# A third place for block outputs, denser last groups and fifteen moved steps in a hand-ordered mixture-of-experts kernel

## The chip, the cores and the metric

The kernel runs on one core of one Trainium2 chip. The metric is the device time of one execution in microseconds, as the median of three executions.

## What is computed

The input is 16 images of 128 channels and 32 x 32 points, in float32. Each image goes through a linear-attention block and then, point by point (token by token), through a mixture of eight experts:

```
x = x + rmsnorm(W_out @ attention(rmsnorm(ln_c(x))) + b_out)   # 4 heads of 32, softmax of q over dims, of k over tokens
t = tokens(x)                                                  # 16 * 1024 tokens of 128
probs = softmax(ln_t(t) @ gate_w + gate_b)                     # 8 experts
cw = the two largest probs of each token, at their experts, else 0
t = t + sum_e cw[:, e] * (gelu(ln_t(t) @ W1[e] + b1[e]) @ W2[e] + b2[e])   # 128 -> 256 -> 128
```

## The kernel before

**Stages.** An image is handled in three stages. In the *attention* (image n) the image is transposed, normed, multiplied and gated; VectorE ends it with `pick` (the two experts and their shares), `place` (row numbers: `row_of`, L936), and GpSimd then sends each token's normed row twice, to the region of each of its two experts in DRAM (`send`, L485: 16 indirect DMAs of 128 rows per image). Two images are a *group*; after the second, VectorE's `table` step (`make_plan`) computes from the counts which 256-row blocks there are and which expert each has. There are 8 groups and at most 23 blocks in each, 184 in all, numbered through: group 6 has 138 to 160, group 7 has 161 to 183. A *block* q goes through: load of rows and of the expert's weights by SyncE (`load_block`, L388 and L392), transpose on TensorE (`turn_block`, L1098), copy on ScalarE (`take_xt`, L588), `up` (L1107), two `gelu` (L594), `down` (L1117), `take_y` on VectorE (L991), store by SyncE to `rows_out` (`store_block`, L401). At last each image's rows come back: GpSimd's `fetch` (L499, 16 indirect DMAs per image), `weigh` on ScalarE (L581, two multiplications per pair of fetches), two adds per half image on VectorE (`add_rows`, L1000 and L1001), transposes on TensorE (`join`, L1027), a copy on ScalarE (`take_out`, L602), and a store of the half image (L407).

**The order.** Every engine runs one queue, written out by hand: a loop over quarter units (`ticks`) goes through all steps, and a step is put into its engine's queue at the unit that the tables give it. A unit delays nothing by itself; it only decides what stands before what in each queue. Steps of image n are at `START[n]` plus an entry of `PE_SLOT`, `ACT_SLOT`, `DVE_SLOT` or `POOL_SLOT`. Blocks are spread evenly over 42 units per image of the group (`block_slot`), and the steps of a block stand at 0 (`turn`), `XT`, `UP`, `UP + GELU`, `DOWN`, `DOWN + TAKE_Y` and `DOWN + 4` (store) behind its slot, its load 5 units ahead. Fetches are every 42 units per image (`fetch_slot`), the weighings 4 units behind a pair, adds and joins 6 and 8 units behind the last of a half.

**The waits around the change.** `rows_out` has `OUT_BUFS` places, taken by the groups in turn. Before the first store of group p, SyncE waits until every image of the group that had the place is added:

```
if j == 0 and p >= OUT_BUFS:
    wait(sp, s_added, 2 * FIRST[p - OUT_BUFS + 1])
```

A fetch of a group's first image waits until all the group's blocks are stored (`all_stored`). Six blocks are in flight (`RING`): the load of block q waits for the transpose of block q-6 (rows) and for `take_y` of block q-6 (weights). `y_rows` holds two images of fetched rows; a fetch waits for the adds of the image two before. A group's first block load waits for the sends of both its images and for the eight zero tails (`zero_tails`, L370), which wait for the plan.

Of the kernel before, what the change touches and what calls it, by code (L numbers as in the profile page):

```python
# [13 lines left out]
BATCH, CH, TOK = 16, 128, 1024  # L14
# [8 lines left out]
GROUPS = (2,) * 8  # L23
# [4 lines left out]
BLOCKS = tuple(2 * TOK * size // ROWS + EXPERTS - 1 for size in GROUPS)  # L28
BLOCK0 = tuple(sum(BLOCKS[:g]) for g in range(len(GROUPS)))
# [11 lines left out]

RING = 6
VALUES = 4
OUT_BUFS = 2
X1_RING, XF_RING, BACK_RING, YG_RING, OUT_RING = 8, 2, 3, 16, 4


PERIOD = 42
PACE = tuple((0.6, 0.6, 0.6, 0.8)[n] if n < 4 else 1.0 for n in range(BATCH))
START = tuple(int(4 * sum(PERIOD * PACE[m] for m in range(n))) / 4 for n in range(BATCH))  # L50
PE_SLOT = {"X0": 0.25, "X1": 2, "Q0": 15, "Q1": 16.1, "Q2": 16.45, "Q3": 17.55, "Q4": 18.65, "Q5": 20.25, "Q6": 20.85,
           "Q7": 21.95, "KT": 29, "KB": 31, "C": 38, "T0": 40.75, "CT": 41, "T1": 41.75, "M": 43, "F0": 45.75, "F1": 47,
           "F2": 47.5, "count": 84.5}
BANK_OF = {"X0": 2, "X1": 3, "Q0": 3, "Q1": 0, "Q2": 1, "Q3": 2, "Q4": 3, "Q5": 0, "Q6": 1, "Q7": 2, "KT": 0, "KB": 1,
           "C": 0, "T0": 1, "T1": 3, "CT": 0, "M": 0, "F0": 0, "F1": 1, "F2": 2, "count": 1, "Y0": 2, "Y1": 3}
ACT_SLOT = {"x_tok0": 1.75, "x_tok1": 3.25, "qkv": 15.75, "exp_q": 34, "exp_k": 34.75, "q_ch0": 41, "ctx_t": 42,
            "q_ch1": 42.5, "square0": 47, "square1": 48.25, "square2": 49, "exp": 76.5}
DVE_SLOT = {"bn1_0": 3.25, "bn1_1": 5.25, "stats1": 7, "inverse": 11.5, "gx": 25.5, "k_part": 27.25, "q_max": 28.75,
            "q_shift": 30.25, "k_max": 29.25, "k_shift": 31.75, "q_sum": 36, "q_norm": 39.75, "ctx": 40, "mix": 44.5, "root_first": 7.5, "root_a": 50.5, "root_b": 51.25,
            "norm0": 54.5, "norm1": 55, "norm2": 56, "x1": 58, "bn2_0": 59.5, "bn2_1": 59.75, "stats2": 61, "root2_a": 61.25, "root2_b": 61.5,  # L60
            "logits": 67.5, "scores": 72.75, "xf0": 78, "xf1": 79.75, "pick": 82.5, "place": 86.25, "table": 88.75}
POOL_SLOT = {"send": 92}
SEND_STEP = FETCH_STEP = 1.25

LOAD_X = -12
UP, DOWN = 5.25, 10.5
XT, GELU, TAKE_Y = 1, 1.5, 1.75
BLOCK_AFTER, FETCH_AFTER, FETCH_PHASE = 4, 13, 29
SCALE, ADD, JOIN = 4, 6, 8

# [5 lines left out]
def at(n, slot):  # L76

    return START[n] + round(4 * PACE[n] * slot) / 4
# [10 lines left out]
def group_of(n):  # L89

    return max(g for g in range(len(GROUPS)) if FIRST[g] <= n)
# [7 lines left out]
def start_slot(g):  # L99

    last = FIRST[g] + GROUPS[g] - 1
    ready = at(last, POOL_SLOT["send"]) + 2 * TILES * SEND_STEP + BLOCK_AFTER
    return ready if g == 0 else max(ready, start_slot(g - 1) + PERIOD * GROUPS[g - 1])


def block_slot(q):

    g = group_of_block(q)
    return start_slot(g) + int(4 * PERIOD * GROUPS[g] * (q - BLOCK0[g]) / BLOCKS[g]) / 4


def fetch_slot(n):

    g = group_of(n)
    done = start_slot(g) + PERIOD * GROUPS[g] + FETCH_AFTER
    phase = START[BATCH - 1] + FETCH_PHASE
    turn = phase + PERIOD * -((phase - done) // PERIOD)
    if n > FIRST[g]:
        return fetch_slot(n - 1) + PERIOD
    return turn if g == 0 else max(turn, fetch_slot(n - 1) + PERIOD)  # L120
# [9 lines left out]
def bank_order():  # L130

    names = list(PE_SLOT) + ["Y0", "Y1"]
    uses = [(at(n, PE_SLOT[name]), n, names.index(name), name) for n in range(BATCH) for name in PE_SLOT]
    uses += [(JOIN_SLOT[n][h], n, names.index(f"Y{h}"), f"Y{h}") for n in range(BATCH) for h in range(2)]
# [19 lines left out]
def build(nc, x, w_qkv, w_out, b_out, g_norm, g_out, gate_w, gate_b, w1, b1, w2, b2, out):  # L154
# [3 lines left out]
    rows_in = [nc.dram_tensor(f"rows_in{i}", [REGION, CH], F32, kind="Internal").ap() for i in range(2)]  # L158
    rows_out = [nc.dram_tensor(f"rows_out{i}", [MAX_BLOCKS * ROWS, CH], F32, kind="Internal").ap() for i in range(OUT_BUFS)]
    experts = nc.dram_tensor("experts", [EXPERTS * P, WROW], F32, kind="Internal").ap()  # L160

    with ExitStack() as ctx:
# [189 lines left out]
        def _(sp):  # L352
# [42 lines left out]
            def store_block(q):  # L395
                p = group_of_block(q)
                j, r = q - BLOCK0[p], q % RING
                if j == 0 and p >= OUT_BUFS:
                    wait(sp, s_added, 2 * FIRST[p - OUT_BUFS + 1])
                sp.wait_ge(s_yb, q + 1)  # L400
                sp.dma_start(rows_out[p % OUT_BUFS][j * ROWS:(j + 1) * ROWS, :].rearrange("(p s) c -> p (s c)", s=SUB),  # L401
                             yb[:, r, :, :].rearrange("p s c -> p (s c)")).then_inc(s_stored[r], 16)
# [51 lines left out]
        def _(pool):  # L454
# [35 lines left out]
            def fetch(n, i):  # L490
# [6 lines left out]
                if k == 0 and t % HT == 0:  # L497
                    wait(pool, s_added, n * 2 + t // HT + 1 - YG_RING // HT)
                pool.indirect_dma_start(  # L499
                    out=y_rows[:, r, k, :], out_offset=None, in_=rows_out[p % OUT_BUFS][0:BLOCKS[p] * ROWS, :],  # L500
                    in_offset=bass.IndirectOffsetOnAxis(
# [513 lines left out]
        def _(pe):  # L1015
# [14 lines left out]
            def attention(n, g):  # L1030
                for h in [h for h in range(2) if g == at(n, PE_SLOT[f"X{h}"])]:
                    if h == 0:
# [152 lines left out]
```

## Time and profile before

| what | us |
|---|---|
| median of 3 executions | 840.89 (838.65 to 841.69) |
| the profiled execution's own time | 844.55 |
| its span, first to last instruction | 842.7 |
| PE busy | 645.8 (77%) |
| DVE busy | 590.6 (70%) |
| ACT busy | 518.2 (61%) |
| POOL busy | 516.1 (61%) |

PE is TensorE, DVE VectorE, ACT ScalarE, POOL GpSimd, SP (SPq) SyncE, which issues the direct DMAs. A share of busy time is an average over the whole span. The mean granted clock of TensorE was 0.909 of full speed. DMA queues moved 173.45 MB, 206 GB/s in the mean. In the views of waits and of instructions in order of time, the text behind an arrow names what ended the idle time; "issue" is time in which the engine waited for nothing that the profile shows.

### The profile page before, as it was taken

The numbers are of one execution on the slowest core, as the hardware profiler recorded it, in microseconds if no ns is written. First come the engines' busy times: TensorE is split into PE (matmuls) and PEld (weight loads), VectorE is DVE, ScalarE is ACT, GpSimd is POOL, SyncE is SP. The second block draws the span as 40 slices with busy tenths as digits, with TensorE's granted clock in tenths as the row PEclk, the third lists the DMA queues.
The fourth block names the chain that finished last, engine by engine and source line by source line (L and its number), as shares of the span: only waits on it lengthen the run. The fifth ranks groups of instructions, "written<-read, shape, count | busy, mean of one in ns | idle before, by whom it ended". The sixth has DMA issues, their size and how long they took to land.

```text
span 842.7 us, 15573 instructions
## 1 busy us (share of the span) xinstructions
PE 645.8 (77%) x3979; PEld 537.8 (64%) x3979; DVE 590.6 (70%) x2185; ACT 518.2 (61%) x1382; POOL 516.1 (61%) x536
## 2 busy tenths in 40 slices
PE   4647546879998989898989898889888867778511
PEld 2425415767877787778777877787767656667400
DVE  4588996886889788978897989797978652222211
ACT  1433325666768696859695869587858563556532
POOL 1004464352177777777777777777777777776274
PEclk9877777999999999989999999899989989999855
DMA  6500035757687888787777787877777778889421
GB/s 167 143 25 29 26 122 158 218 170 230 196 248 226 269 247 258 221 264 248 244 243 250 252 246 249 254 234 240 244 247 235 237 226 283 258 250 305 138 78 56
DMA packets 120864, 173.45 MB, mean 206 GB/s; under 512 B 20792, under 2 KB 82888, under 8 KB 120776
## 3 DMA queue, kind: packets, MB, share of 16 engines
q1 hardware_dynamic: 103352, 138.65, 53.0%
q0 software_dynamic: 16384, 33.59, 13.5%
q8 instruction: 34, 0.56, 0.3%
q14 instruction: 54, 0.44, 0.2%
q10 hardware_dynamic: 1040, 0.21, 0.1%
HBM read 112.86 MB, written 62.14 MB: 208 GB/s over the span
## 4 chain that ended last, share of the span: by engine, by line
PE 37%; DVE 23%; issue 11%; POOL 11%; ACT 9%; DMA 4%; SPq 3%; POOLq 0%; DVEq 0%; ACTq 0%
PE y_ps L1117 10%; PE ab L1040 9%; PE h_ps L1107 8%; POOL y_rows L499 7%; POOL rows_in L485 3%; PE ab L1052 3%; DMA xb<-rows_in 3%; PE ab L1027 3%; PE t_ps L1098 2%; DVE yb L991 2%; ACT L544 2%; ACT y_rows L581 2%; PE ab L1074 2%; ACT qkv L548 1%; DMA y_rows<-rows_out,row_back 1%
## 5 line engine op out<-in xcount | busy, mean ns | idle before, releaser
L485 POOL DMA_INDIRECT rows_in<-xf_tok,row_of x256 | 258.2, 1008 | 219.9 <-DVE row_of L936 141.8
L499 POOL DMA_INDIRECT y_rows<-rows_out,row_back x256 | 255.6, 998 | 96.7 <-issue 77.2
L1117 PE MATMUL y_ps<-wb,hid 128*128 128x128 f32 x1472 | 207.1, 286 | 48.4 <-DVE yb L991 41.4
L1117 PEld LDWEIGHTS y_ps<-wb,hid 128*128 128x128 f32 x1472 | 193.1, 198 | 78.5 <-ACT hid L594 40.6
L1107 PE MATMUL h_ps<-xt,wb 128*128 128x256 f32 x736 | 200.7, 398 | 0.0
L594 ACT ACTIVATE hid<-h_ps,wb 128x256 f32<-128x256 f32 x368 | 160.0, 476 | 53.6 <-PE h_ps L1107 53.3
L991 DVE TENSOR_TENSOR yb<-y_ps,wb 128x256 f32<-128x256 f32 x184 | 76.9, 418 | 121.9 <-PE y_ps L1117 120.6
L1107 PEld LDWEIGHTS h_ps<-xt,wb 128*128 128x128 f32 x736 | 134.5, 200 | 19.5
L588 ACT ACTIVATE xt<-t_ps 128x256 f32<-128x256 f32 x184 | 71.0, 386 | 106.0 <-PE t_ps L1098 105.3
L1040 PE MATMUL ab<-wqkv_t,x_sb 128*128 128x392 f32 x256 | 107.5, 536 | 20.6 <-DVE gate_f L763 16.1
L581 ACT ACTIVATE y_rows<-y_rows,share 128x128 f32<-128x128 f32 x256 | 88.7, 403 | 34.0 <-DMA y_rows<-rows_out,row_back 34.0
L539 ACT ACTIVATE qkv<-ab,root 128x392 f32<-128x392 f32 x128 | 73.2, 588 | 51.6 <-PE ab L1040 26.6
L1098 PE MATMUL t_ps<-ident,xb 128*128 128x128 f32 x368 | 74.4, 285 | 20.8 <-DMA xb<-rows_in 17.8
L1040 PEld LDWEIGHTS ab<-wqkv_t,x_sb 128*128 128x128 f32 x256 | 48.3, 207 | 43.7 <-DVE gate_f L763 19.3
L1098 PEld LDWEIGHTS t_ps<-ident,xb 128*128 128x128 f32 x368 | 47.0, 146 | 30.9 <-DMA xb<-rows_in 22.7
L1000 DVE TENSOR_TENSOR x_tok<-x_tok,y_rows 128x512 f32<-128x512 f32 x32 | 22.2, 695 | 48.9 <-ACT y_rows L581 48.7
L1027 PE MATMUL ab<-ident,x_tok 128*128 128x128 f32 x128 | 22.3, 302 | 43.2 <-DVE x_tok L1001 43.2
L1052 PE MATMUL ab<-qkv 128*128 128x129 f32 x256 | 39.2, 316 | 12.7 <-ACT qkv L548 12.7
L1027 PEld LDWEIGHTS ab<-ident,x_tok 128*128 128x128 f32 x128 | 16.6, 155 | 48.3 <-DVE x_tok L1001 46.3
L1052 PEld LDWEIGHTS ab<-qkv 128*128 128x128 f32 x256 | 36.6, 227 | 16.2 <-ACT qkv L548 16.0
L1074 PE MATMUL ab<-mix,q_ch 128*128 128x136 f32 x256 | 37.2, 286 | 1.5 <-DVE mix L749 1.1
L760 DVE SCALAR_TENSOR_TENSOR x_tok<-ab,root,g_out_bc 128x128 f32<-128x128 f32 x128 | 37.1, 341 | 0.0
(174 smaller groups left out, 883.7 us busy)
## 6 DMA issues: line engine op xcount, KB each, us to landing
wb<-experts SPq DMA_DIRECT2D x184, 321.0 KB
xb<-rows_in SPq DMA_DIRECT2D x184, 128.0 KB, 3.5
rows_out<-yb SPq DMA_DIRECT2D x184, 128.0 KB
rows_in<-zeros SPq DMA_DIRECT2D x78, 128.0 KB, 2.3
x_sb<-in_x_dram SPq DMA_DIRECT2D x16, 512.0 KB, 4.9
out_dram<-out_sb SPq DMA_DIRECT2D x32, 256.0 KB, 4.0
rows_in<-xf_tok,row_of POOLq DMA_INDIRECT x256
y_rows<-rows_out,row_back POOLq DMA_INDIRECT x256, 4.0
```

Of the source, the lines that this page charges most:

```text
L485: pool.indirect_dma_start(out=rows_in[group_of(n) % 2], out_offset=bass.IndirectOffsetOnAxis(ap=row_of[:, n % X1_RING, k, t:t + 1], axis=0 ...
L499: pool.indirect_dma_start(out=y_rows[:, r, k, :], out_offset=None, in_=rows_out[p % OUT_BUFS][0:BLOCKS[p] * ROWS, :], in_offset=bass.Indir ...
L539: act.activation(qkv[:, t, 0:QKV], ab[:, BANK_OF[f"Q{t}"], 0:QKV], ACT.Copy, scale=root[:, 0, t:t + 1]).then_inc(s_qkv, 1)
L581: act.activation(y_rows[:, r, i, :], y_rows[:, r, i, :], ACT.Copy, scale=share[:, n % X1_RING, i, t:t + 1]).then_inc(s_scaled, 1)
L588: act.activation(xt[:, q % 2, :], t_ps[:, 0:ROWS], ACT.Copy).then_inc(s_xt, 1)
L594: act.activation(hid[:, q % 2, k, :], h_ps[:, q % 2, k * ROWS:(k + 1) * ROWS], ACT.Gelu, bias=wb[:, q % RING, B1_COL + k:B1_COL + k + 1]). ...
L991: dve.tensor_tensor(yb[:, q % RING, :, :], y_ps[:, 0:ROWS].rearrange("p (s c) -> p s c", c=CH), wb[:, q % RING, B2_COL:B2_COL + CH].unsque ...
L1040: pe.matmul(claim(n, f"Q{t}")[:, 0:QKV], x_sb[:, n % 2, t * P:(t + 1) * P], wqkv_t[:, :], start=True, stop=True).then_inc(s_qkv_mm, 1)
L1052: last = pe.matmul(bank[:, 0:P + 1], qkv[:, t, K_COL:V_COL], qkv[:, t, V_COL:QKV + 1], start=t == 0, stop=t == TILES - 1)
L1098: last = pe.transpose(t_ps[:, i * P:(i + 1) * P], xb[:, r, i, :], ident[:, :])
L1107: last = pe.matmul(h_ps[:, q % 2, k * ROWS:(k + 1) * ROWS], wb[:, r, k * P:(k + 1) * P], xt[:, q % 2, :], start=True, stop=True)
L1117: last = pe.matmul(y_ps[:, i * P:(i + 1) * P], hid[:, q % 2, k, i * P:(i + 1) * P], wb[:, r, HIDDEN + k * CH:HIDDEN + (k + 1) * CH], start ...
```

## The change

A third `rows_out` place; the blocks of the last two groups spread over 72 and 60 units instead of 84 each; the fetches of images 11 to 15 at units of their own (counted from `START[15]`) instead of 42 apart; and fifteen steps of the tables moved by 0.25 to 2 units.

```diff
-OUT_BUFS = 2
+OUT_BUFS = 3
-PE_SLOT = {... "Q0": 15, ... "count": 84.5}
+PE_SLOT = {... "Q0": 15.25, ... "count": 84.25}
-ACT_SLOT = {"x_tok0": 1.75, ...
+ACT_SLOT = {"x_tok0": 1.25, ...
-DVE_SLOT = {... "stats1": 7, "inverse": 11.5, ... "root_b": 51.25, ... "place": 86.25, "table": 88.75}
+DVE_SLOT = {... "stats1": 7.25, "inverse": 13.5, ... "root_b": 51.5, ... "place": 86, "table": 87.75}
+LAST_SPANS = (72, 60)
+SPAN = tuple(PERIOD * size for size in GROUPS[:-len(LAST_SPANS)]) + LAST_SPANS
+LAST_FETCH = {11: 111, 12: 133, 13: 159, 14: 180, 15: 200}
-XT, GELU, TAKE_Y = 1, 1.5, 1.75
+XT, GELU, TAKE_Y = 1.75, 1.75, 1.75
     (start_slot)
-    return ready if g == 0 else max(ready, start_slot(g - 1) + PERIOD * GROUPS[g - 1])
+    return ready if g == 0 else max(ready, start_slot(g - 1) + SPAN[g - 1])
     (block_slot)
-    return start_slot(g) + int(4 * PERIOD * GROUPS[g] * (q - BLOCK0[g]) / BLOCKS[g]) / 4
+    return start_slot(g) + int(4 * SPAN[g] * (q - BLOCK0[g]) / BLOCKS[g]) / 4
     (fetch_slot)
+    if n in LAST_FETCH:
+        return START[BATCH - 1] + LAST_FETCH[n]
-    done = start_slot(g) + PERIOD * GROUPS[g] + FETCH_AFTER
+    done = start_slot(g) + SPAN[g] + FETCH_AFTER
```

By the tables, the fetches of images 11 to 15 stood at units 684, 726, 768, 810 and 852 and now stand at 682, 704, 730, 751 and 771. Group 6 starts at unit 608.25 in both; group 7 at 692.25 before and at 687 now.

## Rows read from the trace of the kernel before

**Rows 1.** The page: shares of the span, and DMA issues with KB and landing.

```profile
PE 645.8 (77%) x3979; PEld 537.8 (64%) x3979; DVE 590.6 (70%) x2185; ACT 518.2 (61%) x1382; POOL 516.1 (61%) x536
...
wb<-experts SPq DMA_DIRECT2D x184, 321.0 KB
...
y_rows<-rows_out,row_back POOLq DMA_INDIRECT x256, 4.0
```

**Rows 2.** GpSimd in order of time: start, length, [idle time before, releaser].

```profile
227.49 0.96 POOL L485 DMA_INDIRECT rows_in<-xf_tok,row_of  x1 [31.90 <-DVE row_of L936]
...
652.40 1.00 POOL L485 DMA_INDIRECT rows_in<-xf_tok,row_of  x1 [1.04 <-issue]
...
693.50 1.00 POOL L485 DMA_INDIRECT rows_in<-xf_tok,row_of  x1 [0.30 <-issue]
...
713.82 0.97 POOL L499 DMA_INDIRECT y_rows<-rows_out,row_back  x1 [0.31 <-issue]
...
732.66 0.94 POOL L499 DMA_INDIRECT y_rows<-rows_out,row_back  x1 [0.30 <-issue]
734.93 0.94 POOL L499 DMA_INDIRECT y_rows<-rows_out,row_back  x1 [1.33 <-DMA rows_out<-yb]
...
774.60 0.94 POOL L499 DMA_INDIRECT y_rows<-rows_out,row_back  x1 [0.30 <-issue]
793.40 1.00 POOL L499 DMA_INDIRECT y_rows<-rows_out,row_back  x1 [17.86 <-DMA rows_out<-yb]
...
832.34 0.94 POOL L499 DMA_INDIRECT y_rows<-rows_out,row_back  x1 [0.30 <-issue]
```

**Rows 3.** The chain of work that ended last, from 640 us: start, length, what.

```profile
790.71 1.69 DMA rows_out<-yb
...
837.11 1.13 PE ab L1027 x4
```

**Rows 4.** SyncE's queue in order of time: start, length.

```profile
697.50 5.01 SPq L370 DMA_DIRECT2D rows_in<-zeros  x8
...
719.68 0.33 SPq L388 DMA_DIRECT2D xb<-rows_in  x1
...
738.82 0.33 SPq L401 DMA_DIRECT2D rows_out<-yb  x1
```

**Rows 5.** VectorE in order of time.

```profile
691.30 0.18 DVE L936 CAST row_of<-row_f 128x16 int32<-128x16 f32 x1
...
728.81 0.75 DVE L1000 TENSOR_TENSOR x_tok<-x_tok,y_rows 128x512 f32<-128x512 f32 x1 [4.18 <-ACT y_rows L581]
...
730.21 0.42 DVE L991 TENSOR_TENSOR yb<-y_ps,wb 128x256 f32<-128x256 f32 x1
734.46 0.42 DVE L991 TENSOR_TENSOR yb<-y_ps,wb 128x256 f32<-128x256 f32 x1 [3.83 <-PE y_ps L1117]
...
738.11 0.69 DVE L1001 TENSOR_TENSOR x_tok<-x_tok,y_rows 128x512 f32<-128x512 f32 x1
...
786.50 0.42 DVE L991 TENSOR_TENSOR yb<-y_ps,wb 128x256 f32<-128x256 f32 x1 [1.55 <-PE y_ps L1117]
788.27 0.42 DVE L991 TENSOR_TENSOR yb<-y_ps,wb 128x256 f32<-128x256 f32 x1 [1.35 <-PE y_ps L1117]
...
790.27 0.41 DVE L991 TENSOR_TENSOR yb<-y_ps,wb 128x256 f32<-128x256 f32 x1
```

**Rows 6.** ScalarE in order of time, one weighing of image 11.

```profile
728.09 0.69 ACT L581 ACTIVATE y_rows<-y_rows,share 128x128 f32<-128x128 f32 x2 [2.71 <-DMA y_rows<-rows_out,row_back]
```

**Rows 7.** Who waited for whom: us in total, times, longest.

```profile
SPq L401 <- DVE x_tok L1001: 25.0, 6, 4.3
...
ACT y_rows L581 <- DMA y_rows<-rows_out,row_back: 34.0, 21, 3.0
```

**Rows 8.** Stretches: busy us (instructions) of each engine, TensorE clock, DMA share, GB/s.

```profile
742.00:776.00 34.00, 26.41 (x181) 24.02 (x182) 7.74 (x16) 19.75 (x55) 25.61 (x27) 1.00 0.94 300
...
770.00:780.00 10.00, 6.75 (x47) 5.97 (x45) 1.27 (x3) 4.16 (x11) 4.32 (x5) 1.00 0.99 321
```

More of the change, by code:

```diff
@@ L50 @@
 START = tuple(int(4 * sum(PERIOD * PACE[m] for m in range(n))) / 4 for n in range(BATCH))
-PE_SLOT = {"X0": 0.25, "X1": 2, "Q0": 15, "Q1": 16.1, "Q2": 16.45, "Q3": 17.55, "Q4": 18.65, "Q5": 20.25, "Q6": 20.85,
+PE_SLOT = {"X0": 0.25, "X1": 2, "Q0": 15.25, "Q1": 16.1, "Q2": 16.45, "Q3": 17.55, "Q4": 18.65, "Q5": 20.25, "Q6": 20.85,
            "Q7": 21.95, "KT": 29, "KB": 31, "C": 38, "T0": 40.75, "CT": 41, "T1": 41.75, "M": 43, "F0": 45.75, "F1": 47,
-           "F2": 47.5, "count": 84.5}
+           "F2": 47.5, "count": 84.25}
@@ L54 @@
 BANK_OF = {"X0": 2, "X1": 3, "Q0": 3, "Q1": 0, "Q2": 1, "Q3": 2, "Q4": 3, "Q5": 0, "Q6": 1, "Q7": 2, "KT": 0, "KB": 1,
            "C": 0, "T0": 1, "T1": 3, "CT": 0, "M": 0, "F0": 0, "F1": 1, "F2": 2, "count": 1, "Y0": 2, "Y1": 3}
-ACT_SLOT = {"x_tok0": 1.75, "x_tok1": 3.25, "qkv": 15.75, "exp_q": 34, "exp_k": 34.75, "q_ch0": 41, "ctx_t": 42,
+ACT_SLOT = {"x_tok0": 1.25, "x_tok1": 3.25, "qkv": 15.75, "exp_q": 34, "exp_k": 34.75, "q_ch0": 41, "ctx_t": 42,
             "q_ch1": 42.5, "square0": 47, "square1": 48.25, "square2": 49, "exp": 76.5}
-DVE_SLOT = {"bn1_0": 3.25, "bn1_1": 5.25, "stats1": 7, "inverse": 11.5, "gx": 25.5, "k_part": 27.25, "q_max": 28.75,
-            "q_shift": 30.25, "k_max": 29.25, "k_shift": 31.75, "q_sum": 36, "q_norm": 39.75, "ctx": 40, "mix": 44.5, "root_first": 7.5, "root_a": 50.5, "root_b": 51.25,
+DVE_SLOT = {"bn1_0": 3.25, "bn1_1": 5.25, "stats1": 7.25, "inverse": 13.5, "gx": 25.5, "k_part": 27.25, "q_max": 28.75,
+            "q_shift": 30.25, "k_max": 29.25, "k_shift": 31.75, "q_sum": 36, "q_norm": 39.75, "ctx": 40, "mix": 44.5, "root_first": 7.5, "root_a": 50.5, "root_b": 51.5,
@@ L60 @@
             "norm0": 54.5, "norm1": 55, "norm2": 56, "x1": 58, "bn2_0": 59.5, "bn2_1": 59.75, "stats2": 61, "root2_a": 61.25, "root2_b": 61.5,
-            "logits": 67.5, "scores": 72.75, "xf0": 78, "xf1": 79.75, "pick": 82.5, "place": 86.25, "table": 88.75}
+            "logits": 67.5, "scores": 72.75, "xf0": 78, "xf1": 79.75, "pick": 82.5, "place": 86, "table": 87.75}
 POOL_SLOT = {"send": 92}
 SEND_STEP = FETCH_STEP = 1.25
+LAST_SPANS = (72, 60)
+SPAN = tuple(PERIOD * size for size in GROUPS[:-len(LAST_SPANS)]) + LAST_SPANS
```

## Prediction

> **What bounds the kernel now.** I read the shares first, then the clock and transfer share by stretch, then the waits of GpSimd, its instructions in order of time, and last the chain that ended last. No engine is busy over 77% of the span and GpSimd shows only 61% [rows 1]; its queue is nevertheless what sets the end. Each image costs it 16 indirect sends and 16 indirect fetches, and one of them takes 0.94 to 1.0 us with 0.30 us of issue behind it, so 1.25 us, and some are stretched: from the send at 652.40 to the fetch at 713.82 are 48 of them, 1.28 us each [rows 2]. The last long idle time ahead of one of its instructions is 31.9 us before the send of image 4 at 227.49; from there to 775.5 (end of the last fetch of image 13, issued at 774.60) the gaps over 0.4 us are three: 1.04 us twice (before the sends of images 12 and 14, the second is shown) and 1.33 us [rows 2]. Then it stands idle for 17.86 us until the last group's blocks are in DRAM, and fetches images 14 and 15 from 793.40 to 833.3. The span ends 9.4 us later, at 842.7: landing, the two adds, the transposes (837.11), a copy and a store [rows 3].
>
> So the end is 227.5 (first part) + 548.0 (GpSimd without a stop) + 17.9 (the gap) + 39.9 (two images) + 9.4 = 842.7 us. The only idle term is the gap.
>
> What fills it is the last group's 23 blocks (161 to 183). The first of them is loaded at 719.68, when the sends of image 15 (GpSimd turns from them to fetches at 713.82) have landed; its result is taken only at 734.46, the last at 790.27 [rows 4, 5]. Three holes lie between. (a) ScalarE and VectorE work in order: the weighing of image 11 (L581; its fourth pair at 728.09) and its first add (L1000, begun at 728.81 after 4.18 us of waiting) stand ahead of group 6's last `take_y` at 730.21, and group 7 queues behind [rows 5, 6]. (b) The first store of group 7 must wait until image 11 is added, because the two places for block outputs are taken in turn: result at 734.46, store at 738.82, straight after the add begun at 738.11 ends; SP's next block loads stand behind it [rows 4, 5]. (c) SP handles the plan and eight zero tails at 697.50 to 702.5 between two loads of group 6 [rows 4].
>
> **The change, part by part.** A planned unit only orders each queue, it delays nothing; so only the orders and the waits count.
>
> *Three places.* Group p's first store waits for group p−3's images instead of p−2's. In group 7 that is image 9 (fetched by 651.4) in place of image 11: hole (b), 738.82 − 734.9 = 3.9 us, goes. In groups 2 to 6 the same wait holds SP (25.0 us in 6 waits in all, longest 4.3 [rows 7]), but GpSimd has no gap there to give back: worth 0.
>
> *Group 6 in 72 units, group 7 in 60.* All of group 6's blocks now come before the first weighing of image 11 on ScalarE, and its last `take_y` before the first add. With nothing between them blocks follow at 1.8 to 2.0 us (786.50, 788.27, 790.27 [rows 5]); SP's plan step moves from ahead of block 155's load to behind block 157's. I expect group 6 done near 718, not 730. That gives GpSimd only the 1.33 − 0.30 = 1.0 us ahead of image 12's fetch, as its queue is full until 733.6 anyway. Block 161's load can't be earlier than 719.7: it waits for the sends.
>
> *Own places for the last five fetches.* GpSimd's order does not change at all (a fetch never passes a send), nor do the two waits of its queue. What changes is the order on ScalarE, VectorE, TensorE and SP: weighings of images 11, 12 and 13 now stand between the blocks of group 7, about one of an image's eight ahead of each block. On ScalarE one weighing of a pair of fetches stands ahead of each block, so the block pace becomes the fetch pace, 2 × 1.25 = 2.5 us, and the order reads: `xt163` and `gelu161` behind the third weighing of image 11, `gelu177` behind the first of image 13, `gelu183` behind the seventh. Fetch 11 starts at 713.8; its third pair is issued by 720.1 and lands 4.0 us later [rows 1], so block 161's result is at 724 + 0.7 + 0.5 + 0.9 + 0.9 = about 727, 7.5 us earlier than 734.46. At the other end VectorE has `take_y` of block 183 behind *both* adds of image 13. This is what ends last. In the trace a second add ends 738.80, 5.2 us after the last fetch of that image (732.66 + 0.94) [rows 2, 5]. Fetch 13 would end at 775.5 − 1.0 (above) − a part of the two 1.04 us gaps. Those two stand before sends, which need the gate's `row_of`; `count` and `place` move ahead of some of TensorE's and VectorE's work, which gives back between 0 and 2 × 0.74 = 1.5 us, I take 0.7. So: 775.5 − 1.7 = 773.8; add done 779.0; block 183's result there; from its start to the next fetch it took 793.40 − 790.27 = 3.1 us: 782.1. I put 0.9 us on it for landings under fuller queues (the fourth weighing of image 11 shows 2.71 us of waiting for its transfer [rows 6]): 783.0 against 793.4, that is −10.4 us.
>
> Can the blocks keep up? From 727 to 779 are 22 steps, 2.36 us each. Before, the same 22 steps took 790.27 − 734.46 = 55.8 us, 2.54 each, with hole (b) and other queue waits in them; without (b) it is 51.9, or 2.36. Transfers: 23 loads of 321 KB of weights and 128 KB of rows (256 rows of 128 floats) are 10.6 MB, 25 stores of 128 KB 3.3, 43 fetches of 64 KB 2.8, five halves of outputs of 256 KB 1.3, together 18.0 MB [rows 1]. The stretches with fullest queues moved 321 GB/s at a share of 0.99 and 300 at 0.94 [rows 8]. At 321 that is 56 us, at 300 60 us: from 719.7 to 775.8 or 779.7, less about 2 us for stores after the last load, and some 4 us of compute behind it: 777.8 to 781.7. So the transfers are as near as the adds: bound from 779.0 up to 781.7, and 2.7 us more is the upper end of this term.
>
> The Trainium skill (DMA: Bandwidth & Descriptors, section Specifications) gives about 358 GB/s as the limit of a core's HBM traffic. No row here moves more than 321 GB/s, and that at a share of 0.99. By the page's figure the 18.0 MB would be an estimated 50 us and the transfers no bound at all, so the adds alone would decide; by the row they are level with them. That sentence changes nothing in the sum.
>
> *The fifteen steps.* `inverse`, `root_b`, `stats1`, `Q0`, `x_tok0`, `XT`, `GELU` move by 0.25 to 2 units. The work in the first 227 us is the same and these are swaps of neighbours in each queue (`inverse` behind two more normings, `table` of group 0 ahead of four statistics of image 3). From both sides: a gain or a loss of 2 us in 227, value 0. In the steady stretch `xt` and `gelu` now stand behind more of the attention's steps and behind `weigh`s. What hides a late weighing is how early `row_of` is: 2.0 us for image 15 (691.30 + 0.18 against 693.50), nothing for images 12 and 14, whose gaps show it [rows 2, 5]. Where that cover is gone, each us is paid in full. Bounds −2 to +3, value 0. `count` of image 15 now stands behind block 153's transpose, and `place` behind add 10.0; the fetch of image 10 paces both as before, 691 either way.
>
> **Sum.** −1.7 (GpSimd's gaps) − 8.7 (long gap 17.9 to 9.2) = −10.4 us. In the profiled execution's time: 844.55 − 10.4 = 834.2 us, span 832.3. That execution is 3.66 us above the median of the runs, 840.89; the difference carried to the median gives **830.5 us**.
>
> **Rivals.**
> 1. *Transfers set the pace of group 7.* For: 0.94 to 0.99 share in the stretches with both kinds of traffic [rows 8]. Against: 321 GB/s is above the 18.0 MB / 59 us = 305 that the adds ask for. Block 183 at 784 to 786, fetch 14 at 787 to 789, −4.5 to −6.5: 834.5 to 836.4.
> 2. *More comes back*: the swaps bring image 4's send 2 us earlier, both small gaps go, landings stay at 4 us: 825 to 828. For: that send waited for its `row_of` (31.9 us of idle time [rows 2]). Against: nothing in the first part is removed.
> 3. *Slower: `row_of` falls behind GpSimd.* One mechanism: `xt` and `gelu` now queue behind weighings that wait for a fetch (34.0 us in 21 waits already [rows 7]), blocks slip, VectorE's `take_y` holds the gate's steps, and the send starts late. It decides where `row_of` comes after the queue's own end, as for images 12 and 14 now. At 1.4 us for each of the 11 images 5 to 15 it costs 15.4 us; with the 10.4 back at the end the time is 840.89 + 5.0 = 845.9. At half of it, 7.7, it is 838.2, no change.
> 4. *The last store is not what the gap waits for*, and it stays at 17.9: 839.9 with only the 1.0 us. Against: the row names it [rows 2].
>
> **Numbers.** Forecast 0.55; rival 1 0.20; rival 2 0.11; rival 3 0.11 (0.06 of it slower, 0.05 no change or a small gain); rival 4 0.03. Range 825.0 to 837.0. A measurement can tell about 0.5% (4.2 us) from no change: faster is below 836.7. Faster 0.86, no change 0.08, slower 0.06.
>
> **What would show it.** GpSimd's long gap at 8 to 10 us, naming the store of the blocks, its last fetch of image 13 ending near 774; block 183's `take_y` starting within 0.5 us after the second add of image 13; no wait of a `rows_out` store on L1001; first result of group 7 near 727; 300 GB/s or more between 730 and 775. Wrong if GpSimd shows gaps before sends between 270 and 690 (rival 3), if a transfer instead of the add precedes block 183 (rival 1), or if group 6 isn't stored before 733.

## The result, and the profile after

The changed kernel takes 839.40 us (median of 20 executions, 833.44 to 842.11) against 841.47 (20, 838.65 to 847.21) for the kernel before: ratio 0.9955 with the 95% interval 0.9938 to 0.9972, a gain of 3.8 us. Forecast were 830.5 us (825 to 837); the time lies above that range, and the gain is clear of noise (the interval lies below 1) and inside the 0.5% called no change. The profiled execution took 840.95 us, its span 839.2 (before 844.55 and 842.7). Line numbers are those of before plus 5. The diff changes ten entries of the tables (`Q0`, `count`, `x_tok0`, `stats1`, `inverse`, `root_b`, `place`, `table`, `XT`, `GELU`); these are what the text ahead calls fifteen steps, and what is called the moved steps below. The page of the kernel after, the two lines that answer to [rows 1]:

```profile
span 839.2 us, 15572 instructions
...
PE 639.6 (76%) x3979; PEld 527.5 (63%) x3979; DVE 590.0 (70%) x2185; ACT 517.1 (62%) x1382; POOL 517.5 (62%) x536
```

GpSimd of the kernel after, in order of time (columns as in [rows 2]):

```profile
224.29 0.96 POOL L490 DMA_INDIRECT rows_in<-xf_tok,row_of  x1 [29.82 <-DVE row_of L941]
...
711.32 0.97 POOL L504 DMA_INDIRECT y_rows<-rows_out,row_back  x1 [0.31 <-issue]
...
731.69 0.94 POOL L504 DMA_INDIRECT y_rows<-rows_out,row_back  x1 [0.31 <-issue]
...
770.45 0.94 POOL L504 DMA_INDIRECT y_rows<-rows_out,row_back  x1 [0.30 <-issue]
789.75 0.94 POOL L504 DMA_INDIRECT y_rows<-rows_out,row_back  x1 [18.36 <-DMA rows_out<-yb]
...
828.76 0.94 POOL L504 DMA_INDIRECT y_rows<-rows_out,row_back  x1 [0.31 <-issue]
```

Against [rows 2]: image 4's send starts 3.2 us earlier (224.29 for 227.49); from it to the end of fetch 13 are 547.1 us for 548.0, the small gaps gone (0.31 before the fetch at 731.69 where 1.33 stood). The second trace of the kernel before (before_again, below) has neither of the two gaps of 1.04 us, 0.73 us in place of 1.33, and 548.7 us, so those gaps belonged to one execution. And **the long gap is 18.36 us for 17.86**. 3.2 + 0.9 − 0.5 are the 3.5 us between the spans, to rounding. Of the 8.7 us forecast from the end of the kernel, this trace shows nothing.

VectorE of the kernel after:

```profile
718.85 0.42 DVE L996 TENSOR_TENSOR yb<-y_ps,wb 128x256 f32<-128x256 f32 x1 [4.20 <-PE y_ps L1122]
...
727.50 0.42 DVE L996 TENSOR_TENSOR yb<-y_ps,wb 128x256 f32<-128x256 f32 x1 [0.67 <-PE y_ps L1122]
...
736.18 0.69 DVE L1005 TENSOR_TENSOR x_tok<-x_tok,y_rows 128x512 f32<-128x512 f32 x1 [4.54 <-ACT y_rows L586]
736.91 0.69 DVE L1006 TENSOR_TENSOR x_tok<-x_tok,y_rows 128x512 f32<-128x512 f32 x1
737.52 0.42 DVE L996 TENSOR_TENSOR yb<-y_ps,wb 128x256 f32<-128x256 f32 x1
...
784.16 0.69 DVE L1006 TENSOR_TENSOR x_tok<-x_tok,y_rows 128x512 f32<-128x512 f32 x1
784.77 0.42 DVE L996 TENSOR_TENSOR yb<-y_ps,wb 128x256 f32<-128x256 f32 x1
```

These are, in order: the last result of group 6 (718.85, before 730.21), the first of group 7 (727.50, before 734.46), the second adds of image 11, the result of block 164 right behind them, the last add of image 13 and the result of block 183 (784.77, before 790.27) [rows 5]. The front of group 7 came when the forecast said. The rest did not: the first load of group 7 is at 714.3 (719.7 before), its last result at 784.8 (790.3), and the time between is 70.5 us where it was 70.6. The blocks stand 2.61 units apart in the order instead of 3.65, and took as long as before. The long gap is 9.2 us over the forecast 9.2: block 183's result came 5.8 us later than 779.0, from it to the next fetch it took 5.0 us instead of 4.0, and fetch 13 ended 2.4 us earlier (771.4 for 773.8).

ScalarE, the third weighing of image 11, its eighth (the adds at 736.18 wait for it) and the last of image 13; and on GpSimd the second of the two fetches that the third weighing waits for:

```profile
722.77 0.69 ACT L586 ACTIVATE y_rows<-y_rows,share 128x128 f32<-128x128 f32 x2 [2.46 <-DMA y_rows<-rows_out,row_back]
...
735.46 0.69 ACT L586 ACTIVATE y_rows<-y_rows,share 128x128 f32<-128x128 f32 x2 [2.51 <-DMA y_rows<-rows_out,row_back]
...
782.71 0.69 ACT L586 ACTIVATE y_rows<-y_rows,share 128x128 f32<-128x128 f32 x2
```

```profile
717.60 0.94 POOL L504 DMA_INDIRECT y_rows<-rows_out,row_back  x1 [0.30 <-issue]
```

TensorE around the hole at block 164, and one `down` at full clock:

```profile
738.08 2.05 PE L1122 MATMUL y_ps<-wb,hid 128*128 128x128 f32 x8 [3.47 <-DVE yb L996]
...
748.38 1.06 PE L1122 MATMUL y_ps<-wb,hid 128*128 128x128 f32 x8
```

Stretches of the kernel after (columns as in [rows 8]):

```profile
730.00:740.00 10.00, 6.43 (x40) 5.67 (x39) 2.14 (x4) 5.17 (x16) 7.56 (x9) 0.85 0.89 231
740.00:750.00 10.00, 9.44 (x53) 8.11 (x52) 1.80 (x5) 6.19 (x18) 7.56 (x9) 0.81 0.80 245
...
760.00:770.00 10.00, 7.83 (x54) 6.58 (x53) 2.54 (x5) 5.40 (x16) 7.56 (x9) 1.00 0.98 300
770.00:780.00 10.00, 9.94 (x70) 8.72 (x70) 3.51 (x7) 8.04 (x24) 1.09 (x2) 1.00 0.86 276
```

Who waited for whom on SyncE's queue, 700 to 792 us (us in total, times, longest), and the store that opens the gap's end, from the chain:

```profile
SPq L397 <- DVE yb L996: 11.1, 7, 3.0
SPq L406 <- DVE yb L996: 9.9, 8, 2.0
```

```profile
785.21 3.54 DMA rows_out<-yb
```

Four suspects can be read from this. (1) *Transfers*: 300 GB/s at a share of 0.98 between 760 and 770; but the other stretches from 730 to 780 have 231 to 288, below the 300 that the forecast named as its sign, and in the last one TensorE is the busy one, 9.94 of 10 us. (2) *The hole at block 164*: a weighing waits 2.51 us for its fetch, the adds behind it 4.54 us, block 164's result stands behind the adds, TensorE stands still for 3.47 us and then runs its eight matmuls in 2.05 us instead of 1.06, at a granted clock of 0.81 to 0.85 in the mean of the stretch (at 748.38 the same eight take 1.06 us again, the full clock, 2.4 GHz; 2.05 us is the lower level, 1.2 GHz). The kernel before has such a dip too, 0.83 over 730 to 740. (3) *SyncE*: it reads every block's addresses from the plan, four blocks at a time, in register loads of about a microsecond. (4) *The ring*: the weights of block q are loaded only when the result of block q−6 is taken (L397, 11.1 us of waiting in 7 waits). A block passes 17.25 units from load to result; at 60 / 23 = 2.61 units apart that is 6.6 blocks, more than the six places. At the 3.65 units of before it was 4.7.

### The profile page after: what moved, and what is told of

Same layout as the page of the kernel before. It is cut to its first block and busy times, and to the rows that moved or that the text cites. A ratio compares the mean times of both kernels' runs of the same rounds, so it can differ in the third digit from the quotient of the medians.

```text
span 839.2 us, 15572 instructions
## 1 busy us (share of the span) xinstructions
PE 639.6 (76%) x3979; PEld 527.5 (63%) x3979; DVE 590.0 (70%) x2185; ACT 517.1 (62%) x1382; POOL 517.5 (62%) x536
## 3 DMA queue, kind: packets, MB, share of 16 engines
q0 software_dynamic: 16384, 33.59, 13.4%
## 5 line engine op out<-in xcount | busy, mean ns | idle before, releaser
L1122 PE MATMUL y_ps<-wb,hid 128*128 128x128 f32 x1472 | 204.3, 283 | 48.8 <-DVE yb L996 41.4
L1122 PEld LDWEIGHTS y_ps<-wb,hid 128*128 128x128 f32 x1472 | 188.2, 196 | 76.0 <-ACT hid L599 42.3
L599 ACT ACTIVATE hid<-h_ps,wb 128x256 f32<-128x256 f32 x368 | 160.9, 476 | 67.4 <-PE h_ps L1112 65.6
L1112 PE MATMUL h_ps<-xt,wb 128*128 128x256 f32 x736 | 193.9, 387 | 0.3 <-ACT hid L599 0.3
L1112 PEld LDWEIGHTS h_ps<-xt,wb 128*128 128x128 f32 x736 | 130.7, 195 | 17.5 <-issue 0.5
L593 ACT ACTIVATE xt<-t_ps 128x256 f32<-128x256 f32 x184 | 71.0, 386 | 43.5 <-PE t_ps L1103 38.2
L1032 PEld LDWEIGHTS ab<-ident,x_tok 128*128 128x128 f32 x128 | 16.1, 153 | 49.5 <-DVE x_tok L1006 48.2
```

The source lines that it names most:

```text
L593: act.activation(xt[:, q % 2, :], t_ps[:, 0:ROWS], ACT.Copy).then_inc(s_xt, 1)
L599: act.activation(hid[:, q % 2, k, :], h_ps[:, q % 2, k * ROWS:(k + 1) * ROWS], ACT.Gelu, bias=wb[:, q % RING, B1_COL + k:B1_COL + k + 1]). ...
L1112: last = pe.matmul(h_ps[:, q % 2, k * ROWS:(k + 1) * ROWS], wb[:, r, k * P:(k + 1) * P], xt[:, q % 2, :], start=True, stop=True)
L1122: last = pe.matmul(y_ps[:, i * P:(i + 1) * P], hid[:, q % 2, k, i * P:(i + 1) * P], wb[:, r, HIDDEN + k * CH:HIDDEN + (k + 1) * CH], start ...
```

## Experiments

All times in one table. The ratio is to the kernel before, run on the same chip in turns, and the ratios are what may be compared: the kernel before had 841.47 us beside after, 841.60 beside steps_only, tail_only, places_only and after_again, 842.33 beside half_weights, fixed_addresses, add_later and ring7, 843.84 beside before_again, ring7_before, ring7_half and ring7_shift, and 843.23 beside the last four. In half_weights, ring7_half and fixed_addresses the blocks of group 7 work on other numbers. The trace columns come from one execution each: start of image 4's send; load of block 161 to result of block 183; mean step from block 164 to 183; the long gap.

| kernel | median us (n) | ratio [95%] | send 4 | 161 to 183 | step | gap |
|---|---|---|---|---|---|---|
| before | 841.47 (20) | 1 | 227.5 | 70.6 | 2.57 | 17.9 |
| before_again | 842.56 (10) | 0.9994 [0.9964, 1.0025] | 226.5 | 71.3 | 2.55 | 18.9 |
| after | 839.40 (20) | 0.9955 [0.9938, 0.9972] | 224.3 | 70.5 | 2.49 | 18.4 |
| after_again | 839.64 (12) | 0.9964 [0.9939, 0.9988] | 225.0 | 69.1 | 2.44 | 15.3 |
| steps_only | 840.04 (12) | 0.9968 [0.9946, 0.9990] | 224.5 | 69.6 | 2.47 | 16.1 |
| tail_only | 841.17 (12) | 0.9979 [0.9957, 1.0002] | 228.4 | 67.2 | 2.34 | 14.9 |
| places_only | 841.43 (12) | 0.9986 [0.9959, 1.0014] | 225.3 | 69.9 | 2.43 | 18.4 |
| half_weights | 835.65 (10) | 0.9926 [0.9898, 0.9953] | 223.9 | 65.8 | 2.31 | 12.9 |
| fixed_addresses | 835.53 (10) | 0.9910 [0.9880, 0.9939] | 224.4 | 67.7 | 2.27 | 12.1 |
| add_later | 840.76 (10) | 0.9977 [0.9948, 1.0007] | 223.3 | 69.8 | 2.65 | 17.3 |
| ring7 | 834.83 (8) | 0.9919 [0.9888, 0.9949] | 224.6 | 65.7 | 2.29 | 12.1 |
| ring7_before | 842.32 (10) | 0.9996 [0.9971, 1.0021] | 223.9 | 69.0 | 2.47 | 15.7 |
| ring7_half | 831.68 (4) | 0.9866 [0.9837, 0.9895] | 224.3 | 63.4 | 2.26 | 9.3 |
| ring7_shift | 835.18 (4) | 0.9882 [0.9836, 0.9928] | 225.2 | 64.9 | 2.32 | 12.2 |
| load_later | 840.93 (12) | 0.9969 [0.9949, 0.9989] | 225.1 | 70.1 | 2.59 | 18.4 |
| ring8 | 834.10 (6) | 0.9879 [0.9850, 0.9908] | 223.2 | 67.4 | 2.41 | 13.0 |
| ring7_again | 833.71 (6) | 0.9883 [0.9856, 0.9910] | 224.4 | 64.8 | 2.28 | 12.4 |
| ring7_shift_again | 832.33 (6) | 0.9857 [0.9823, 0.9891] | 224.1 | 63.7 | 2.28 | 10.8 |

### Which part carries the gain

**steps_only**: the kernel before with the moved steps alone.

```diff
 (before) PE_SLOT, ACT_SLOT, DVE_SLOT, XT and GELU as in the change; OUT_BUFS, spans and fetches as before
```

> Only the fifteen moved steps, everything else as before. Theory A (the whole gain of the change comes from the moved steps, by way of an earlier start of GpSimd's unbroken queue): the send of image 4 starts near 224.3 us instead of 227.5, the 1.04 us gaps before the sends of images 12 and 14 go, GpSimd's long gap stays at 17 to 19 us, the time is 3 to 4 us below before (ratio 0.995 to 0.997). Theory B (the denser tail gives the gain): the send of image 4 may start earlier, but the time is within 1 us of before.

**tail_only**: the change without the moved steps.

```diff
 (after) PE_SLOT, ACT_SLOT, DVE_SLOT and XT, GELU as before
```

> Three places, the denser last two groups and the own places of the last five fetches, without the fifteen moved steps. Theory A: the send of image 4 starts at 227.5 as before, GpSimd's long gap is 17 to 19 us, the time is within 1 us of before. Theory B: the long gap falls to 14 or less and the time is 3 to 4 us below before. The prediction as put: gap near 9, time 8 to 10 us below before.

**places_only**: the kernel before with three places.

```diff
-OUT_BUFS = 2
+OUT_BUFS = 3
```

> Three places for block outputs and nothing else. The store of group 7's first block no longer waits for the adds of image 11 (3.9 us in the trace of before). If that wait set the last group's end, the long gap of GpSimd shrinks by up to 3.9 us and the time with it; if the group's pace is set by its own queues (theory A), the time is within 1 us of before.

**after_again**: the changed kernel once more, beside these.

> The changed kernel itself, to stand beside the three parts on the same chip. Theory A: the same as the moved steps alone to within 1 us. Theory B: 3 us or more below them.

Measured: the steps alone 0.9968, all of it 0.9964 beside them, the tail alone 0.9979 and the places alone 0.9986, the last two with 1 inside the interval. So the steps alone give what the whole change gives, as near as can be measured; for the tail and the places no gain of their own is shown, and the intervals of some ±0.2% don't allow a finer split: that of the tail alone reaches over that of the steps alone. The long gap of tail_only, 14.9 us, lies between what the two theories asked for. The first send of GpSimd's queue after its long wait, with and without the steps:

```profile
224.47 0.96 POOL L485 DMA_INDIRECT rows_in<-xf_tok,row_of  x1 [29.15 <-DVE row_of L936]
```

```profile
228.41 0.96 POOL L490 DMA_INDIRECT rows_in<-xf_tok,row_of  x1 [31.33 <-DVE row_of L941]
```

steps_only shows 224.47, tail_only 228.41. In all 13 traces of kernels with the steps it lies from 223.2 to 225.2 (mean 224.3), in the five without from 223.9 to 228.4 (mean 226.3): 2.0 us of the 2.7 that the steps gain by the ratio, though the two ranges overlap. The long gap, in contrast, is 16.9 us in the mean of the five traces with six places in the ring and the dense tail (14.9 to 18.4) and 17.4 in the five with the old tail (15.7 to 18.9). Which of the steps does it was not tried. The single long gap is not a steady number: 18.4 and 15.3 in two executions of the changed kernel. What is compared below is therefore the time first, and the trace for its place.

### What holds the blocks of group 7

**half_weights**: the loads of group 7 bring half the columns of the weights, which takes about 3.8 of the 18 MB away. The other half of the tile keeps what an earlier block left, so the engines do the same work on other numbers.

```diff
+cols = B2_COL + CH if p < len(GROUPS) - 1 else (B2_COL + CH) // 2
-sp.dma_start(wb[:, r], ...)
+sp.dma_start(wb[:, r, 0:cols], experts[..., 0:cols])
```

> The changed kernel, with only half of each expert's weight row loaded for the blocks of group 7 (164 KB in place of 329 KB, 3.8 MB of about 18 MB less; the other half keeps what an earlier block left there, so the output isn't the reference's). Theory T (transfers set the pace of group 7): from the load of block 161 to the result of block 183 it takes 60 us or less instead of 69 to 70, and GpSimd's long gap falls from 15 to 18 us to 8 or 9. Theory Q (queue order and SyncE's waits set it, not bytes): 67 us or more, gap 14 or more.

Measured: 0.9926, the stretch 65.8 us, gap 12.9. Fewer bytes help, by 0.3% or 2.4 us against the changed kernel's ratio (0.9955), with intervals that overlap at the edge; yet the stretch did not fall to the 60 us expected of bytes as the only cause, nor did it stay at the 67 of the other theory: another limit lies close behind.

**fixed_addresses**: in group 7 the addresses are constants (expert by block number) instead of register loads from the plan, so its blocks work on other rows than the plan's.

```diff
+if p == len(GROUPS) - 1:
+    rows[0] = [(j % EXPERTS) * CAP] * VALUES
+    rows[1] = [(j % EXPERTS) * P] * VALUES
-if j % VALUES == 0:
+elif j % VALUES == 0:
```

> The changed kernel, with fixed row and expert addresses for the loads of group 7 in place of those read from the plan (same bytes and number of transfers; the blocks compute on other rows, so the output isn't the reference's). SyncE then loads no registers between these loads (about 1 us for each of two or three reads in four blocks). Theory S (SyncE's own work sets the pace): 161 to 183 takes 62 us or less, gap 11 or less. Theory T or Q: 67 us or more, gap as before within 2 us.

Measured: 0.9910, gap 12.1, the stretch 67.7. That is neither theory: the stretch is that of the second, the gap nearly that of the first, because block 161's result came later behind its load (17.0 us for 13.2) and the 22 steps behind it faster (2.30 us for 2.60). By the ratios SyncE's register loads cost 3.8 us (0.9955 to 0.9910), if the other addresses made nothing faster; that is not shown, since they also change which rows and weights are read, and this run has the highest rate of all (342 GB/s between 750 and 760). The number of bytes is the same, so transfers were not full all the time. With the register loads gone SyncE waits 21.8 us for results six blocks back, where it waited 11.1 us before: the ring takes over. The two register loads of one such step, from the chain of the kernel after:

```profile
756.10 1.11 SPq L364
757.25 0.99 SPq L364
```

**add_later**: the hole at block 164 closed by moving the second add (and join) of image 11 six units later.

```diff
+ADD_SLOT[11][1] += 6
+JOIN_SLOT[11][1] += 6
```

> The changed kernel with the second add and join of image 11 moved 6 units later, behind the results of two or three more blocks in VectorE's queue. In the changed kernel the result of block 164 waited there until 737.5, 6.3 us after that of block 163, and TensorE then ran at the lower clock for some 4 us. Theory Q: block 164 is done by 733 to 734, no such hole, and block 183 and the long gap come 3 us or more earlier. Theory T: block 164 is earlier, block 183 is not (within 1.5 us).

Measured: block 164's result at 734.5 instead of 737.5, block 183's at 784.9 as before (784.8), gap 17.3, ratio 0.9977. The hole is real and worth nothing: 3.0 us won in front are gone 19 blocks later, at 2.65 us a block.

**ring7**: seven blocks in flight, nothing else.

```diff
-RING = 6
+RING = 7
```

> The changed kernel with seven blocks in flight instead of six. In its order a block's load stands 5 units ahead of its slot and its result 12.25 behind, 17.25 units, which is 6.6 blocks at 60/23 = 2.6 units: the load of weights waits for the result six blocks back (11.1 us of SyncE waiting in 7 waits in group 7). Theory R (this ring sets the pace): these waits go and 161 to 183 takes 63 us or less, gap 12 or less. Theory T: the waits go, the time from 161 to 183 stays at 67 us or more.

Measured: 0.9919, 834.83 us, gap 12.1, the stretch 65.7; again, beside other kernels, 0.9883 with 12.4 and 64.8. The stretch lies between the two theories (63 or less, 67 or more), so the ring is a limit and not the only one. The waits of the weight load, which were 11.1 us in 7, in the trace of ring7 (SyncE, 700 to 792 us):

```profile
SPq L397 <- DVE yb L996: 4.0, 1, 4.0
```

**ring7_before** (the same line in the kernel before) and **before_again** (that kernel unchanged).

> The kernel before with seven blocks in flight instead of six. At its spacing of 3.65 units a block spans 17.25 units in the order, 4.7 blocks, so a ring of six is deep enough by the order. Theory R2 (the ring costs something only at the dense spacing): the time within 1.5 us of before, 161 to 183 within 1 us of before (70 us). If the ring hides slow transfers at any spacing: 3 us or more below before, as for the changed kernel.

> The kernel before, once more, for its trace. Its first trace was an execution 3.7 us above the median of its runs, with block 183's result at 790.3 us and a long gap of GpSimd of 17.9 us. Theory N (part of the room that the prediction saw was that one execution): now block 183 at 785 to 788, and the send of image 4 anywhere from 225 to 228.5. If the trace is typical instead: 789.5 or later.

Measured: 0.9996 and 0.9994. At the wide spacing of before a seventh place brings nothing that can be measured: the ring became a limit by the change. The pace of before, 2.57 us, thus had another cause, which was not looked for. That kernel's second trace has block 183's result at 790.9 and the gap at 18.88, so its first was no odd execution.

**ring7_half**: seven in flight and half the weights' columns in group 7, to see whether the two are one limit or two.

> The changed kernel with seven blocks in flight and half of the weight bytes in group 7 (its output isn't the reference's for that). Neither ring nor bytes can then hold the blocks. Theory P (TensorE's own work, 2.0 us a block and 0.44 us a join, is the floor from block 164 on, and block 164 waits for the second add of image 11): from the second add of image 11 to the result of block 183 it takes 40 to 43 us, as for each of the two alone (44.0 and 43.5), and no less. If transfers still held each of the two: 38 us or less.

Measured: 831.68 us, 0.9866 (four executions), gap 9.33, the stretch 63.4. By the time it can't be told whether the two add up, as the interval reaches over that of ring7. By the trace they don't: from the result of block 164 to that of 183 it is 47.3 us in the kernel after, 43.9 with half the weights, 43.5 with seven places and 42.9 with both. That is what the expectation put down to TensorE's own work as the floor. VectorE of this kernel where the group ends, and GpSimd behind it:

```profile
774.20 0.69 DVE L1006 TENSOR_TENSOR x_tok<-x_tok,y_rows 128x512 f32<-128x512 f32 x1
774.93 0.69 DVE L1007 TENSOR_TENSOR x_tok<-x_tok,y_rows 128x512 f32<-128x512 f32 x1
775.53 0.42 DVE L997 TENSOR_TENSOR yb<-y_ps,wb 128x256 f32<-128x256 f32 x1
```

```profile
778.48 0.94 POOL L505 DMA_INDIRECT y_rows<-rows_out,row_back  x1 [9.33 <-DMA rows_out<-yb]
```

This is the end that was forecast: block 183 right behind the last add of image 13, this time without late blocks ahead of it, 6.4 us after that image's last fetch (769.1), 2.9 us to the fetch of image 14, a gap of 9.3 (forecast 9.2). The mechanism was there to be had, once two limits were away: the ring, which the forecast had not priced, and bytes, which it had priced too low. What is left is TensorE, busy 9.39 of 10 us, the transfers at 0.76:

```profile
760.00:770.00 10.00, 9.39 (x70) 8.80 (x70) 3.46 (x7) 8.17 (x25) 7.02 (x8) 1.00 0.76 223
```

**load_later**: is it the depth of the ring, or SyncE blocked by the wait with stores and other loads behind it? The loads move from 5 to 3 units ahead, so that the result stands ahead of the load in the order.

```diff
-if g == BLOCK_SLOT[q] - 5:
+if g == BLOCK_SLOT[q] - (5 if q < BLOCK0[-1] else 3):
```

> The changed kernel, ring of six, with the loads of group 7 standing 3 units ahead of their slots instead of 5, so that a block spans 15.25 units in the order, 5.85 blocks: SyncE then meets the result of six blocks back before it meets the load. Theory QS (the cost is SyncE standing blocked, with stores and other loads behind it): the waits on L397 fall from 8 to 11 us to under 3, block 183 2 to 3 us earlier, as with a ring of seven. Theory D (too few blocks in flight for the time of a round from result to load to result): the waits go too, but block 183 comes within 1 us of the changed kernel (784.8) or later.

**ring8**: eight in flight.

> The changed kernel with eight blocks in flight. With seven, two stretches of 10 us moved 323 and 324 GB/s at a share of 1.00. Theory D: transfers have taken over, block 183 and the time within 1 us of the ring of seven. If depth alone still decided: another 2 to 3 us less.

Measured: load_later 0.9969 with the gap at 18.41 and block 183 at 786.1, no different from the kernel after, though its blocks span 15.25 units, 5.85 blocks, and fit into six places by the order. But its weight loads still wait, so it took only part of the blocking away, and does not settle the question:

```profile
SPq L397 <- DVE yb L996: 8.9, 5, 2.8
```

Beside it ring7_again has 833.71 us for 840.93, its slowest execution (835.74) below the fastest of load_later (836.46). ring8 gives 834.10 (0.9879) beside 833.71 (0.9883) for ring7_again: the eighth place brings nothing, although this wait no longer occurs in group 7 at all. With a seventh place the transfers are full. Stretches of ring7, and a fetch in its chain:

```profile
750.00:760.00 10.00, 7.70 (x54) 6.64 (x53) 3.10 (x7) 7.36 (x22) 7.56 (x9) 1.00 1.00 324
760.00:770.00 10.00, 9.39 (x69) 8.50 (x68) 2.20 (x5) 5.97 (x18) 7.56 (x9) 1.00 1.00 323
```

```profile
752.26 6.08 DMA y_rows<-rows_out,row_back
```

**ring7_shift**, and again: seven in flight and the weighings, adds and joins of images 11 to 15 six units later, so that blocks stand ahead of them.

```diff
+LATER = {n: 6 for n in range(11, 16)}
-    ... FETCH_SLOT[n][2 * t + 1] + SCALE
+    ... FETCH_SLOT[n][2 * t + 1] + SCALE + LATER.get(n, 0)
 (ADD_SLOT[n][h] and JOIN_SLOT[n][h] of these images += 6)
```

> The changed kernel with seven blocks in flight, and all steps of images 11 to 15 behind their fetches (weighing, adds, joins, copies, stores) 6 units later in the order, that is behind two more blocks of group 7. Theory P: block 161 comes 3 us or more earlier against its load than with seven blocks alone (14.9 us), the second add of image 11 holds no block up to 165, block 183 is 2 to 4 us earlier, and so is the end: 2 to 4 us below seven blocks alone. If transfers hold them (324 GB/s at a share of 1.00 with seven blocks): block 183 within 1.5 us of it.

> The changed kernel with seven blocks in flight, again, beside the others on the same chip: 0.990 to 0.993 of before.

> Seven in flight and the steps of images 11 to 15 6 units later, again. Its traces showed block 183 no earlier than with seven alone (783.0 against 782.0), so the time should be the same to within 1.5 us, and the 0.9882 of the first measurement (four runs) an accident of few runs. If the order does help: 2 us or more below seven alone.

Measured: 0.9882 the first time and 0.9857 the second, where ring7 alone has 0.9883 beside it. Its intervals reach over those of ring7, so the shift is not shown to help. GpSimd at the end of the gap in the second:

```profile
781.76 0.94 POOL L509 DMA_INDIRECT y_rows<-rows_out,row_back  x1 [10.77 <-DMA rows_out<-yb]
```

The lowest time of a kernel that computes the whole is this one, at 832.33 us against 843.23 for the kernel before beside it (0.9857 [0.9823, 0.9891]). Seven in flight, with or without the shift, beats both kernels.

## Why the prediction was wrong

**The step that failed** is "Can the blocks keep up?". It took 2.36 us a block from the time of before less hole (b), found the transfers at 777.8 to 781.7, near the adds at 779.0, and let the adds decide. From 727.5 to 784.8 it was 2.60 us a block, 22 times 0.24 = 5.3 us more than taken, and that is most of the 5.8 us by which block 183 was late. Behind it stand two errors. One is that a stretch with a hole in it was priced as if taking away the hole left the rest. Load to last result stayed at 70.5 us; places_only took hole (b) away (block 161 at 728.9), ended at 69.9 and had 2.59 us a block from there, where 2.36 was taken; add_later closed the next one and gained nothing. The pace over 19 blocks was set by something that none of these holes touch. The other is that the check went by one resource, bytes, and by its full rate, where the stretches from 730 to 780 moved 231 to 300 GB/s. Relieved one at a time, bytes give 2.4 us, register loads 3.8 and a ring place 3.0 and 6.1 (ratios 0.9926, 0.9910, 0.9919 and 0.9883 against 0.9955, times 841.5). The first three intervals touch that of the changed kernel at its edge; ring7_again and ring7_half lie clear of it. So no one of them is "the" bound: with six places the load of a block's weights can't start before the result six blocks back; at the pace measured one round from result over load issue, landing and transpose to result is an estimated 6 × 2.5 = 15 us (block 161 took 13.2 from load to result), and what lengthens the round (bytes under way, SyncE's register loads) is paid in the pace. That last is an argument that fits the experiments; no run shows it by itself. The order gives a hint of the ring, 17.25 / 2.61 = 6.6 against six, and I had not worked it out; load_later, at 5.85, shows that the quotient alone doesn't decide.

Point by point:

- *Three places, hole (b) gone, group 6 done near 718, first result of group 7 near 727*: right in the number (718.85 and 727.50), the second by luck in part: the sixth fetch of image 11 began 2.5 us earlier than counted on (717.60 for 720.1), 5.2 us passed to the third weighing instead of 4, and 4.7 from there to the result instead of 3. *Block 161's load not before 719.7*: it came at 714.3. Of the 5.4 us, 2.5 are GpSimd's queue, which ran earlier (its first fetch of image 11 at 711.32 for 713.82); why the load then stood 3.0 us behind that fetch instead of 5.9 isn't known. They did not help the first result, because `gelu` of block 161 stands behind the third weighing of image 11 (722.77), as the forecast had it.
- *Weighings between blocks, pace 2 × 1.25 = 2.5 us*: this number, named in passing and dropped for 2.36, was the measured one (2.49, 2.44). That need not be its reason: with a seventh place the same order ran at 2.29.
- *Block 183 behind both adds of image 13*: right in place (784.16, then 784.77), wrong in what sets it. The adds were to come 5.2 us behind the last fetch; they came 13.4 behind it (12.0 in the second trace), since the last weighing (782.71, with no idle time ahead of it) stood in ScalarE's queue behind late blocks. I had looked at the last add, and not at image 11's, which stands ahead of block 164 in the same way.
- *3.1 + 0.9 us from the last result to the fetch*: 5.0 and, in the second trace, 3.3. The last store took 3.54 us to land, 1.69 before [rows 3]; why isn't known.
- *GpSimd's small gaps, −1.7*: 548.0 to 547.1, so −0.9, of gaps that the second trace of before doesn't have; over all traces this stretch lies from 544.9 to 549.4, and no tenth of it means anything.
- *Moved steps at 0, bounds −2 to +3*: −2.7 us by steps_only, just outside, with an interval from −0.8 to −4.5. By the medians this was most of the gain; the tail's own part can't be told from nothing.
- *Median against profiled execution*: 3.66 us were carried over from three executions; over twenty the median of before is 841.47, so the base was 0.6 us low, and the profiled execution of the kernel after lies only 1.55 us above its median. Of the 8.9 us between 830.5 and 839.4, 6.8 stand in the profiled execution (840.95 for 834.2) and 2.1 come from carrying 3.66 over.

**The rivals.** Rival 1 had the place (block 183 at 784 to 786, fetch 14 at 787 to 789; measured 784.8 and 789.75, 788.06 in the second trace) and, of its cause, a part: with half the weights' bytes the stretch is 65.8 us, still 6.5 more than the 59.3 taken. Its time, 834.5 to 836.4, also kept the first part's gain at nothing and the base low. Of rival 2 the earlier send of image 4 came, the small gaps went, and the median landing of a fetch stayed near 4 us (4.1); its time did not come, since it counted on the forecast's end as well. Rival 3, the slower case, did not occur: from 224 to 771 us no gap of GpSimd stands before a send, and `row_of` of image 15 was there at 687.0 for a send at 690.9. Rival 4 has the time (839.9) and the gap (18.4 and 15.3) and not the cause, so its number is luck: the gap still names the store of the last blocks, and ring7_half shows it follows them down to 9.3.

The page *DMA: Bandwidth & Descriptors* (section Specifications) of the Trainium skill has about 358 GB/s as the HBM limit of a core. No run here reaches it: stretches of 10 us at a share of 1.00 or more moved 303 to 342 GB/s (both in fixed_addresses, 760 to 770 and 750 to 760; 335 in before_again, 770 to 780). The lower figure of the trace was the better one to plan with; it was just not the only bound.

**Open.** What makes up the rest of the stretch at seven and eight places (64.8 to 67.4 us) is not told apart finer than transfers at 1.00 and TensorE near 9.4 of 10 us in turn. Why the first send scatters by up to 4.5 us without the moved steps isn't known. Whether the tail alone, apart from the steps, gives its 0.2% lies below what was resolved.

## What to carry to other kernels

Before steps are put closer in a hand-written order, divide the distance from load to release by the new spacing. When it exceeds the places in the ring, suspect the ring and try one place more: here it was worth 3 to 6 us behind the change (6.6 blocks in six places), and nothing without it (4.7). Fitting the order into the ring by loading later (5.85) gained nothing, so it is the place that helps, and not the quotient. Price a stretch by what each resource needs per step, all of them, and not by its old length less the holes seen in it; a hole ahead of a limit is slack. And when an instruction stands last behind an add, ask what the add itself stands behind.

## What was not expected of the hardware

- Stretches at a share of 1.00 or more moved 303 to 342 GB/s with block loads, stores and indirect fetches mixed; in one of them (ring7, 324 GB/s) an indirect fetch took 6.08 us to land, against a median of 4.5 in that trace.
- Reading a block's addresses into SyncE's registers takes about 1 us a load (1.11 and 0.99), and taking them out of 23 blocks, with other addresses read, was worth 0.45% (0.9955 to 0.9910).
- After TensorE had stood still for 3.47 us, eight matmuls took 2.05 us instead of 1.06, and the granted clock of the two stretches around was 0.85 and 0.81. That cost nothing that add_later could win back (0.9977).
- Between two executions of one kernel the gap moved by 3.0 us (18.36 and 15.34; 1.7 of it between the last result and the next fetch, 1.3 in the end of fetch 13) while the medians agree to 0.24 us: one trace shows where the time lies, and not how much.
